# An adaLN transformer layer on one core: the last two modulation pieces computed side by side in the first attention step

## The reference

```python
mod = (silu(c) @ wmod).reshape(4, 6, 1, -1)      # wmod is 512 x 3072
sa, ca, ga, sb, cb, gb = (mod[:, k] for k in range(6))
ga = (2 * (ga >= 0) - 1) * maximum(abs(ga), 0.25)
gb = (2 * (gb >= 0) - 1) * maximum(abs(gb), 0.25)
h = layernorm(x) * (1 + ca) + sa
x = x + ga * attention(h)                        # q, k, v, softmax, @ Wo + bo
h = layernorm(x) * (1 + cb) + sb
x = x + gb * moe(h)
```

## Time and profile before

| | |
|---|---|
| median of 3 runs | 1521.27 us |
| the profiled execution, its own time | 1518.95 us |
| its span (first to last instruction) | 1516.8 us |
| PE busy | 1501.2 us, 99% |
| DVE, ACT, POOL busy | 981.2, 729.2, 715.5 us |
| moved by DMA | 311.92 MB, mean 206 GB/s |

### The profile page before, as it was taken

One profiled execution on the slowest core, in us unless ns is written; L12 is line 12 of the kernel. 1 busy time (PEld: TensorE's weight loads), 2 busy tenths in 40 slices (PEclk: granted clock), 3 DMA queues, 4 the chain that ended last, 5 costly groups with the idle time before them and its releaser, 6 DMA issues.

```text
span 1516.8 us, 29264 instructions
## 1 busy us (share of the span) xinstructions
PE 1501.2 (99%) x8812; PEld 1339.7 (88%) x8812; DVE 981.2 (65%) x2213; ACT 729.2 (48%) x1733; POOL 715.5 (47%) x767
## 2 busy tenths in 40 slices
PE   8999999999999999999999999999999999999998
PEld 4788888887899999999999999989989999999997
DVE  6977666677777777777777777785458322222258
ACT  4532222346666666666666666673332233333323
POOL 2113333446766566666565665769822311111154
PEclk9999999999999999999999999999999999999999
DMA  9336555677858486666757486646553555765577
GB/s 330 118 140 229 194 195 194 220 264 240 253 160 249 149 247 190 198 193 202 208 160 238 146 246 179 217 148 242 201 162 153 188 197 193 270 235 204 190 250 234
DMA packets 205632, 311.92 MB, mean 206 GB/s; under 512 B 80673, under 2 KB 142497, under 8 KB 198641
## 3 DMA queue, kind: packets, MB, share of 16 engines
q1 hardware_dynamic: 198432, 287.04, 56.8%
q0 software_dynamic: 5680, 18.62, 4.1%
q10 hardware_dynamic: 1440, 5.24, 0.9%
HBM read 189.97 MB, written 120.88 MB: 205 GB/s over the span
## 4 chain that ended last, share of the span: by engine, by line
PE 86%; POOL 6%; issue 3%; DMA 2%; DVE 1%; ACT 1%; SPq 0%; POOLq 0%; ACTq 0%; DVEq 0%
PE bank L1634 45%; PE bank L1749 18%; PE bank L1864 8%; PE bank L1816 7%; PE bank L1847 4%; PE bank L1918 2%; PE bank L1952 1%; POOL xr L1296 1%; POOL h L1296 1%; DMA keys<-k_ring 1%; DMA acc<-wq 1%; POOL acc L1080 1%; POOL h L1093 0%; POOL acc L1078 0%; POOL h L1095 0%
## 5 line engine op out<-in xcount | busy, mean ns | idle before, releaser
L1634 PE MATMUL bank<-w,xt 128*128 (+2 forms) x1608 | 287.5, 327 | 0.3 <-ACT gate_s L1561 0.2
L1634 PEld LDWEIGHTS bank<-w,xt 128*128 128x128 f32 x1608 | 261.9, 188 | 6.7 <-DVE xt L2300 0.6
L1457 ACT ACTIVATE prob<-prob,row_inv 128x128 f32<-128x128 f32 (+3 forms) x256 | 137.3, 560 | 78.5 <-DVE row_inv L2337 78.3
L2457 DVE TENSOR_TENSOR ht_lo<-bank,ht_hi 128x128 fp32r<-128x128 f32 (+1 forms) x210 | 47.7, 282 | 181.5 <-ACT ht_hi L1577 181.4
L1445 ACT ACTIVATE prob<-bank,neg_max 128x128 f32<-128x128 f32 (+3 forms) x256 | 133.7, 526 | 42.7 <-DVE neg_max L2329 42.5
L1634 PE MATMUL bank<-wv_hi,h_hi 128*128 128x256 f32 x512 | 147.1, 287 | 0.0
L1634 PE MATMUL bank<-wv_hi,h_lo 128*128 128x256 f32 x512 | 144.8, 283 | 0.0
L1634 PE MATMUL bank<-wv_lo,h_hi 128*128 128x256 f32 x512 | 144.7, 283 | 0.0
L1634 PE MATMUL bank<-w,ht_hi 128*128 (+3 forms) x414 | 134.6, 406 | 1.2 <-DVE ht_lo L2457 1.1
L1257 POOL DMA_INDIRECT xin<-ffn_rows,slot_tokens x39 | 39.7, 1019 | 184.7 <-PE bank L1918 180.3
L2324 DVE TENSOR_REDUCE row_max<-bank 128x1 f32<-128x128 f32 (+3 forms) x256 | 119.7, 488 | 6.6
(11 more groups left out here) (260 smaller groups left out, 3885.7 us busy)
## 6 DMA issues: line engine op xcount, KB each, us to landing
keys<-k_ring SPq DMA_DIRECT2D x64, 512.0 KB, 3.3
ch_raw<-wexp SPq DMA_DIRECT2D x128, 170.0 KB, 3.2
experts_hi<-ch_hi SPq DMA_DIRECT2D x128, 170.0 KB, 2.6
experts_lo<-ch_lo SPq DMA_DIRECT2D x128, 170.0 KB, 2.7
w<-experts_hi SPq DMA_DIRECT2D x9, 2176.0 KB, 7.8
w<-experts_lo SPq DMA_DIRECT2D x9, 2176.0 KB, 14.3
q_transposed<-q_out SPq DMA_DIRECT2D x64, 256.0 KB, 2.0
k_even<-keys SPq DMA_DIRECT2D x16, 1024.0 KB, 5.7
```

What stands on the lines that cost most here:

```text
L1457: ins = act.activation(part, part, ACT.Copy, scale=row_inv[:, h, r:r + 1])
L1634: ins = pe.matmul(dst, a, m, start=(k == 0), stop=(k == last))
```

## The change

Pieces 5 and 4 are computed together in the first attention step, where piece 4 alone was. The two chains alternate, their output rows at partitions 0 and 32 of the same bank 7. Piece 5's weights are loaded where they were and kept in `w_x`; piece 4's weights go to `stage[0]`, and their load moves from `half(4)` to `half(25)`, ahead of the load of wv. ACT evicts both rows, and PE's last `weigh` waits for ACT instead of DVE. DVE's clamp of piece 5 moves to the end of the first step, with four instructions for five. SP stores both rows at the end of the first step. The bias rows of batch 0 move from ACT in stage 1 to POOL in the first step, after the two pieces have been computed.

```diff
-MOD_AFTER = {2: 2, 3: 5}
+MOD_AFTER = {2: 2}
-MOD_EV = {0: 1, 1: 2, 3: 3, "raw5": 4, 2: 5, 5: 6, 4: 7}
+MOD_EV = {0: 1, 1: 2, 3: 3, 2: 4, 4: 5, "raw5": 6, 5: 7}
...
@@ SP, half(v)
-                if v == 4:
-                    sp.wait_ge(mod_ev, MOD_EV[5])
-                    mod_weights(4, w_x)
...
                 if v == NV - 3:
+                    sp.wait_ge(sum_ok, 4 * NU)
+                    sp.wait_ge(ul_ok, 2 * NU)
+                    mod_weights(4, stage[0])
                     sp.wait_ge(w_full, 7 * (NV - 2))
...
@@ SP, step
                 if first:
                     store_mod(4)
+                    store_mod(5)
@@ POOL, step
                     pool.wait_ge(kh_ok, 4 * NK)
+                    pool.wait_ge(bo_ld, 16)
                     bias_rows(1)
+                    pool.wait_ge(mod_full, len(MOD_ORDER))
+                    bias_rows(0)
@@ ACT, half(v)
-                    act.wait_ge(mod_full, MOD_ORDER.index(5) + 1)
-                    act.activation(mod_raw5, bank[7][0:B, :], ACT.Copy).then_inc(mod_ev, 1)
...
-                    bias_rows(0)
@@ ACT, step
                 if first:
+                    act.wait_ge(mod_full, len(MOD_ORDER))
+                    act.activation(mod_row[4], bank[7][32:32 + B, :], ACT.Copy, bias=1.0).then_inc(mod_ev, 1)
+                    act.activation(mod_raw5, bank[7][0:B, :], ACT.Copy).then_inc(mod_ev, 1)
                     for e in range(4):
                         act.wait_ge(k_st[e], 16 * ring_uses(e, 4 * NK))
@@ PE
-                if v == 0:
-                    mod_piece(5, w_x, 7)
...
+            def last_pieces():
+                pe.wait_ge(modw_ld[5], 48)
+                pe.wait_ge(modw_ld[4], 64)
+                pe.wait_ge(s_exp, 3)
+                for c in range(DC):
+                    for k, w in enumerate((w_x, stage[0])):
+                        ins = pe.matmul(bank[7][32 * k:32 * k + B, :], c_silu[:, c, :], w[:, c, :],
+                                        start=(c == 0), stop=(c == DC - 1))
+                        if c == DC - 1:
+                            ins.then_inc(mod_full, 1)
...
                 if first:
-                    mod_piece(4, w_x, 7)
+                    last_pieces()
...
                 if first:
-                    pe.wait_ge(mod_ev, MOD_EV[4])
+                    pe.wait_ge(mod_ev, MOD_EV["raw5"])
                 weigh(1)
@@ DVE, step
-                if first:
-                    dve.wait_ge(mod_full, MOD_ORDER.index(4) + 1)
-                    dve.tensor_scalar(mod_row[4], bank[7][0:B, :], 1.0, None, ALU.add).then_inc(mod_ev, 1)
...
                 if not last:
                     invert(0, n + 1)
+                if first:
+                    mod_piece(5)
```

More of the change, by code:

```diff
@@ L313, in adaln_layer @@
         ring = [k_ring[:, e] for e in range(4)]
-        mod_row = {0: q_out[0:B, 2, :], 1: q_out[0:B, 3, :], 3: ct[0][0:B, :], 2: mod_a, 5: mod_a,
+        mod_raw5, mod_a5, mod_s5 = (w_x[0:B, c, :] for c in (1, 2, 3))
+        mod_row = {0: q_out[0:B, 2, :], 1: q_out[0:B, 3, :], 3: ct[0][0:B, :], 2: mod_a, 5: mod_a5,
                    4: acc[0:B, NT - TT, :]}
-        mod_raw5 = w_x[0:B, 0, :]
         xs = [x_in] + [x_later[:, b] for b in range(B - 1)]
@@ L616, in stage1_over @@
             eng.wait_ge(k22_ok, NK)
-            eng.wait_ge(mod_ev, MOD_EV[5])
+            eng.wait_ge(mod_ev, MOD_EV[2])
         def reader(v, k):
@@ L1386, in plain @@
                         t_high(b // 2, (1,))
-            def bias_rows(b):
-                act.activation(acc[:, b * TT:(b + 1) * TT, :], bo_b[:, :].unsqueeze(1).to_broadcast([P, TT, D]),
-                               ACT.Copy).then_inc(acc_ok, 1)
             def half(v):
@@ L1422, in half @@
                         elif e == 3:
-                            act.wait_ge(mod_st, 3 * 16)
+                            act.wait_ge(mod_st, 2 * 16)
                         elif n == 0:
@@ L1641, in _ @@
             pe.wait_ge(silu_c, 1)
-            MOD_FREE = {3: (mod_ev, 1), 2: (modc_ok, 2), 5: reader(0, 1), 4: (s_exp, 3)}
+            MOD_FREE = {3: (mod_ev, 1), 2: (modc_ok, 2)}
             def mod_piece(m, w, to):
                 if m != 1:
-                    pe.wait_ge(modw_ld[m], {5: 48, 4: 64}.get(m, 16))
+                    pe.wait_ge(modw_ld[m], 16)
                 if m in MOD_FREE:
@@ L1694, in _ @@
             PLAIN_FREE = [[None] * 4, [(q_ev, j + 1) for j in range(4)],
-                          [reader(0, 2), reader(0, 3), reader(0, 4), (mod_ev, MOD_EV["raw5"])],
+                          [reader(0, 2), reader(0, 3), reader(0, 4), reader(0, 1)],
                           [reader(0, 5), reader(0, 6), (q_ev, 12), (q_ev, 9)]]
@@ L2091, in link, with mod_piece @@
                 dve.wait_ge(dchain, dc[0])
[L2093 to L2101, removed]
+            def mod_piece(m):
+                src, a, s = (mod_raw, mod_a, mod_s) if m == 2 else (mod_raw5, mod_a5, mod_s5)
+                dve.wait_ge(mod_ev, MOD_EV[3] if m == 2 else MOD_EV["raw5"])
+                link(dve.scalar_tensor_tensor(out=a, in0=src, scalar=-1.0, in1=src, op0=ALU.mult, op1=ALU.max))
+                link(dve.tensor_scalar(a, a, 0.25, None, ALU.max))
+                link(dve.tensor_scalar(s, src, 0.0, 2.0, ALU.is_ge, ALU.mult))
+                dve.scalar_tensor_tensor(out=mod_row[m], in0=s, scalar=-1.0, in1=a,
                                          op0=ALU.add, op1=ALU.mult).then_inc(mod_ev, 1)
@@ L2266, in half @@
                 if v in MOD_AFTER:
-                    m = MOD_AFTER[v]
-                    mod_piece(m, mod_raw if m == 2 else mod_raw5)
+                    mod_piece(MOD_AFTER[v])
                 if v == 0:
@@ L2418, in step @@
                     invert(0, n + 1)
+                if first:
+                    mod_piece(5)
                 if b == 1:
-                    dve.wait_ge(acc_ok, 1 + 3 * TT)
+                    dve.wait_ge(acc_ok, B * TT)
             def add_out(m, b, i):
```

1 line of the change is left out of this document (removed).

## The result

| | before | after |
|---|---|---|
| median, 7 runs each | 1521.27 us | 1527.31 us |
| lowest to highest | 1519.66 to 1522.69 | 1524.3 to 1530.7 |
| predicted | | 1524.7 (1521.0 to 1526.6) |

The ratio is 1.0038, with a 95% interval of 1.0028 to 1.0047: 5.8 us slower (4.3 to 7.1), where 3.4 were predicted. The direction was right, the size was not, and the time lies 0.7 us outside the range. A second profile of each (experiments e11 and e12) gave 1519.12 and 1528.8.

A forecast was written before the change was run, and what follows sets the result against it. The prediction took PE to bound the kernel, with 86% of the chain of waits. Piece 5 (0), side by side (0), weights in the queue (2.9) and second store (0.5) made 3.4 us on 1521.27: 1524.7 us, range 1521.0 to 1526.6.

The forecast's parts named there:

- Piece 5 leaves: In half(0) near 60 us: PE idles 3.2 us waiting for DVE's h; removal worth 0 to 0.1 us, taken as 0.
- Rival 3: PE's gaps at 59 and 370 us lower its clock to 1.2 GHz: 1525.1 to 1526.6 us; chance 0.22.
- The clock elsewhere: At 372 us, behind PE's wait for wo: a clock fall would show 0.8 us, counted only in Rival 3.
- Two pieces for one: At 355 us: both pieces take at most 3.78 us, 0.2 more, which disappears in PE's wait for DVE: 0.
- Rival 4: At 355 us: both chains in one bank take turns, 3.4 us more; 1524.9 us, or 1524.4 alone; chance 0.07.
- The last weigh: At 364.61 us: PE's wait for DVE's eviction goes, 0.2 to 0.4 us gained, hardly any kept since wo is late.
- The load: Piece 4's weights, 1.05 MB, issued near 328.5 us into a full DMA queue, delay wo and PE: 2.9 us.
- Everything queued behind it lands that much later: After piece 4's load near 328.5 us: wv, the last key stores and wo land about 2.9 us later.
- Rival 1: The weights fill gaps of the DMA engines and cost 0: about 1521.9 us; chance 0.25.
- rival 2: The gap left in half(0) is used, 3.5 us of PE work goes, weights also hidden: 1517.8 us; chance 0.08.
- The clamp: DVE's four instructions for piece 5 ending the first step, some 2.3 us, hidden while PE waits for wo: 0.
- the second store: At the end of the first step: two rows stored delay POOL, q and third-step scores, 0.5 us (0.4 to 1.3).

The follow-up runs named there:

- e11: The kernel before, unchanged, profiled a second time, one execution: 1519.12 us.
- e12: The changed kernel, unchanged, profiled a second time, one execution: 1528.8 us.
- e8: The changed kernel with piece 4's load issued by ACT into its own queue, at half(26): ratio 1.0049, median 1528.45 us.
- e10: The changed kernel with q's first load, in 2048 small pieces, moved behind the four key stores of half(26): ratio 1.0040.
- e9: The kernel before, with piece 5's four matmuls in half(0) replaced by a single one of four columns: ratio 1.0004.
- e1: The kernel before, with only the load of piece 4's weights moved to half(25), ahead of wv: ratio 1.0028.
- e2: The changed kernel with piece 5's four matmuls put back into half(0) as filler, their result unused: ratio 1.0032.
- e4: The changed kernel with piece 4's load moved to half(27), and second h parts and first chunks behind the last key stores: ratio 1.0026.
- e5: The changed kernel without the load of piece 4's weights and PE's wait for it, piece 4 computed from other data: ratio 1.0017.
- e6: The changed kernel without piece 4's load, and with piece 5's four matmuls put back into half(0), their result unused: ratio 1.0012.
- e15: The same kernel as e6, unchanged, run once more: ratio 1.0013.
- e14: The kernel before, with one more store of piece 4's row at the end of the first step, POOL waiting for both: ratio 0.9999.
- e13: The kernel of e6 with one DVE instruction in place of the four of piece 5's clamp: ratio 1.0012.
- e7: The changed kernel loading only half of piece 4's weights (two of four chunks, 0.5 MB): ratio 1.0027.

## Why the prediction was wrong

- **Piece 5 leaves, priced at 0 to 0.1.** The gap, its releaser and its length were right; the term was mis-sized, because the clock's fall stood in a rival (3, chance 0.22) and not in the sum. Of nine profiles with the gap, seven show the fall and two (e8, e10) a clock of 1.00 in both windows. In those two the transposes of `plain(2)` begin at 68.66 and 68.74, as in before, in the seven between 69.39 and 70.19. So the gap itself is free, as the prediction had it, and the clock costs what is left behind the transposes: 0.7 us in e9, 0.8 in after, 1.0 to 1.5 in the other five. Rival 3's 0.4 to 1.1 us for this place was about right.
- **The clock elsewhere, 0 in the sum.** Rival 3 looked at the gap at 370 us as well; in after's trace the clock fell behind three waits, for some 10 us in all. In the medians, an estimate: a mean clock of 0.9971 against 0.9993 is some 6.7 us more at the lower level, in which PE does 3.3 us less work; waits hide a part of that. The executions bear it out in part: in after, e8 and e10 those with the lower clock are the slower ones, in e1, e2 and e4 no such order shows. The fastest execution of after, 1524.3 us at 0.999, is 3.0 us above before's median, near the 3.4 of the sum without the clock; one execution can't prove that.
- **Two pieces for one, 0.** Right (3.60 us for eight matmuls). Rival 4 is refuted.
- **The last weigh, gains 0.2 to 0.4, all lost to wo.** Right in kind: no wait there in after, and a wait for wo behind it.
- **The load, 2.9 us.** In the medians right in size: 3.2 (after less e5, with the falls of the clock behind its waits in it), and 2.7 to 5.8 alone (e1). The path was half wrong. "Everything queued behind it lands that much later", and for wv "just hidden, at most 0.4 us", named wv as what delays DVE's sums. wv was indeed late (DVE waited 2.33 us for it), and hidden. What held the scores of the first or the second step was ACT's wait for the ring slots of `half(26)`'s stores, up to 8.18 us, fed by an issue that holds SP for 6.66 to 8.67 us in every trace with the full load and q's pieces ahead of it (six of six), against 2.08 to 5.46 without it (nine). The order in SP's ring, by which the prediction explained the late key stores, isn't needed for it (e8). In after's trace the queue then has a hole (135 GB/s), which an estimate from bytes over bandwidth can't contain; e6 shows that the hole doesn't need the load. In the profiled executions this made the delay at wo 4.3 to 5.7 us, more than the medians bear out; why they lie above the medians stays open. Rival 1, the weights hidden, is refuted (e1's interval begins at 2.7 us), and rival 2 by PE's wait for `h_lo`.
- **The clamp, "now PE stands still for wo beside it: 0", and the second store, 0.5 us.** This is the step that failed, with the clock: 0.5 us for both, and 1.8 to 2.0 measured with load and gap gone (e6, e15). The clamp was taken at 2.3 us from instructions that ran alone; beside POOL's splits it takes 4.6 to 5.1. A second store of a ready row is free (e14). But the first step is held by two chains, the clamp through v and the stores through POOL and q (e15, e13). With the load in, the clamp itself is hidden behind wo in after's trace, as predicted, but the chain of POOL's stores is not: it grows by 2.1 us, of which 0.9 is the two stores (inside the prediction's 0.4 to 1.3), 0.7 the longer issue of q and 0.5 POOL's chunks beside the clamp, and the prediction had neither of the last two. The wait for q at 391.02 was 1.99 us, where about 1 was expected.

In sum: 3.2 (load, predicted 2.9) + 0.8 (gap and its fall of the clock, predicted 0) + 1.8 (rest of the first step, predicted 0.5) = 5.8. These are the steps from after to e5 to e6 to before, so they add up by their making, and the first two are uncertain by about 2 us, the last by 1.4; the traces support the last two more sharply. The later falls of the clock are no fourth term: they sit in the load and in the first step. How much of the 5.8 us they are stays open below the 3.3 us. No version tried is measurably faster than the kernel before.

## What to carry to other kernels

- A gap of 3 us on a saturated TensorE can cost its clock (seven of nine profiles here) even where the idle time itself is free. An instruction group that stands where PE would wait for another engine anyway is free there: moving it away wins nothing. Put the clock into the sum, and compare the granted clock of the executions, not of the profiled one alone.
- A load added to a full queue is not only its bytes: look at what the issuing engine has queued behind the issue that will block, and at who waits for buffers that the blocked stores must leave.
- Price an instruction by a row in which its neighbours run what they will run beside it, and ask of every small instruction moved in front of a critical one what it delays. Before removing the wait that the trace names, look for a second chain that ends at the same time.

## What the hardware showed beside

- DVE instructions on 4 rows of 512 took 0.40 to 0.68 us on their own in stage 1 (before, piece 5's clamp) and 2.13, 2.43, 2.44 and 2.76 us beside POOL's subtraction of 1024 columns (e15, e13, after, e7), where they ended 0.3 to 0.6 us behind it.
- Which queue the load stood in made no difference to SP's block: 8.67 us with it in ACT's queue, issued 2.9 us earlier than in after.
- After a gap of 3.04 to 3.17 us at the same place the granted clock fell in seven executions and not in two. It also fell behind waits of 1.87 and 1.99 us (after).
- One SP issue can take 8.08 us where others take 0.5: directly behind a load in 2048 small pieces, with some 3 MB issued in the 5 us before it (piece 4's weights, wv, keys, q). In after's trace the DMA engines then moved 135 GB/s over 3 us.
